# Attention scores from two float32r parts, with two heads in the row halves of the TensorE array

## The reference

```python
q = _split_heads(Q @ W_Q.T)
k = _split_heads(K @ W_K.T)
v = _split_heads(V @ W_V.T)
scores = jnp.einsum('bhqd,bhkd->bhqk', q, k) / jnp.sqrt(jnp.float32(DK))   # DK = 16
scores = jnp.where(mask == 0, -jnp.inf, scores)                            # layer 0 only
weights = jax.nn.softmax(scores, axis=-1)
attn = jnp.einsum('bhqk,bhkd->bhqd', weights, v)
```

## Time and profile before

| what | value |
|---|---|
| median of three runs | 1252.16 us |
| span of the profiled execution | 1261.0 us |
| TensorE busy | 1114.1 us, 88% |
| VectorE busy | 834.2 us, 66% |
| ScalarE busy | 644.9 us, 51% |
| GpSimd busy | 211.6 us, 17% |
| DMA, SyncE's queue | 128.03 MB, 33.3% of 16 engines' span |
| mean granted TensorE clock | 0.946 |

### The profile page before, as it was taken

How to read it: one execution, slowest core, us unless ns; L and a number is a source line. 1 busy time by engine, 2 the same in 40 slices (tenths; PEclk the granted TensorE clock), 3 DMA queues, 4 the chain that set the end, 5 groups by cost and what they waited for, 6 DMA issues and landing times. The chain is left out here.

```text
span 1261.0 us, 17546 instructions
## 1 busy us (share of the span) xinstructions
PE 1114.1 (88%) x5578; PEld 545.0 (43%) x5578; DVE 834.2 (66%) x2112; ACT 644.9 (51%) x1341; POOL 211.6 (17%) x273
## 2 busy tenths in 40 slices
PE   7889999999897999999859999996979999998480
PEld 4423344434452334333446666664523333335350
DVE  5877777776577898898752222225789898868622
ACT  3446666666442776767513333322437767774240
POOL 3310000000242000010211222202410010102244
PEclk9989999999998999999959999998969999999695
DMA  8963312220069334342470220103953223201154
GB/s 252 317 205 87 88 35 81 52 52 1 1 222 274 89 104 116 93 116 62 169 279 29 102 91 29 27 22 106 330 184 107 76 64 85 64 15 67 30 155 142
DMA packets 102433, 139.38 MB, mean 111 GB/s; under 512 B 10756, under 2 KB 84360, under 8 KB 100936
## 3 DMA queue, kind: packets, MB, share of 16 engines
q1 hardware_dynamic: 98264, 128.03, 33.3%
q0 software_dynamic: 4080, 10.23, 3.0%
HBM read 86.30 MB, written 52.17 MB: 110 GB/s over the span
## 5 line engine op out<-in xcount | busy, mean ns | idle before, releaser
L888 ACT ACTIVATE r<-ps 128x512 f32<-128x512 f32 x768 | 427.8, 600 | 209.4 <-PE ps L973 126.5
L377 DVE TENSOR_REDUCE m<-ps 128x1 f32<-128x512 f32 x512 | 320.7, 683 | 38.1 <-PE ps L960 38.1
L973 PE MATMUL ps<-r 99*128 99x512 bf16 x768 | 293.6, 387 | 11.5 <-ACT r L888 5.8
L960 PE MATMUL ps<-r 96*128 96x512 bf16 x720 | 282.9, 394 | 15.0 <-DVE m L377 5.0
L990 PE MATMUL ps<-r 128*32 128x512 f32 x1536 | 199.4, 606 | 5.9 <-ACT r L888 3.3
L373 DVE CUSTOM_DVE_ANT_0 r<-ps,r 128x512 bf16<-128x512 f32 x256 | 166.6, 688 | 55.2 <-PE ps L960 54.6
L973 PEld LDWEIGHTS ps<-r 99*128 99x128 bf16 x768 | 74.7, 98 | 201.6 <-ACT r L888 114.2
L960 PEld LDWEIGHTS ps<-r 96*128 96x128 bf16 x720 | 71.1, 99 | 110.1 <-DVE m L377 29.1
L864 POOL COPY r<-r 128x256 f32<-128x256 f32 x48 | 19.1, 401 | 526.6 <-PE ps L990 526.6
L977 PE MATMUL ps<-r,identb 128*128 128x512 bf16 x256 | 97.9, 382 | 0.0
L1663 DVE COPY r<-ps 128x512 f32<-128x512 f32 x46 | 31.8, 692 | 90.4 <-PE ps L1710 90.4
(11 more groups left out here) (152 smaller groups left out, 1196.8 us busy)
## 6 DMA issues: line engine op xcount, KB each, us to landing
r<-q_parts SPq DMA_DIRECT2D x48, 384.0 KB, 4.0
r<-k_parts SPq DMA_DIRECT2D x48, 384.0 KB, 5.0
k_parts<-r SPq DMA_DIRECT2D x24, 384.0 KB, 3.2
q_parts<-r SPq DMA_DIRECT2D x24, 384.0 KB, 3.2
r<-in_w SPq DMA_DIRECT2D x16, 512.0 KB, 3.5
r<-in_w SPq DMA_DIRECT2D x8, 1024.0 KB, 14.2
k_parts<-r SPq DMA_DIRECT2D x24, 256.0 KB, 3.2
q_parts<-r SPq DMA_DIRECT2D x24, 256.0 KB, 3.1
```

Source lines behind the costliest of these rows:

```text
L377: ins = dve.tensor_reduce(out, mem.ps[:, bank, :], AX.X, ALU.max)
L888: act.activation(mem.probs[:, u // HG, u % HG, :], ps[:, ST + (UNITS * g + u) % DEEP, :], ACT.Exp, scale=SCALE).then_inc(a.p_exp.sem, 1)
L960: pe.matmul(ps[:, led_bank(n), :], mem.qst[g][0:ROWS, h, t * P:(t + 1) * P], mem.kst[g][0:ROWS, h, :], start=True, stop=True).then_inc(a.s ...
L973: ins = pe.matmul(out, mem.kst[g][0:KROWS, h, kt * P:(kt + 1) * P], mem.qst[g][0:KROWS, h, :], start=True, stop=not a.masked)
```

## The change

```diff
-TERMS = 6
+TERMS = 3
-PARTS = 3
+PARTS = 2
+SIDES = 2
+SIDE = P // SIDES
 def load_stacks(sp, a, b, g):
-        rows = src[b, g * GW:(g + 1) * GW, :, :].rearrange("(h r) t n -> (r t) h n", h=HG)
-        sp.dma_start(dst[0:ROWS, :, :], rows).then_inc(a.stacks[g].sem, 16)
+        rows = src[b, g * GW:(g + 1) * GW, :, :].rearrange("(h j r) t n -> j (r t) h n", h=PAIRS, j=SIDES)
+        for j in range(SIDES):
+            sp.dma_start(dst[j * SIDE:j * SIDE + ROWS, :, :], rows[j]).then_inc(a.stacks[g].sem, 16)
+def led_tile(v):
+    return (v % HG) ^ 1, v // HG
+def stack_of(stack, h, rows):
+    j = h % SIDES
+    return stack[j * SIDE:j * SIDE + rows, h // SIDES, :]
     def rest(b, n):
-        dve.scalar_tensor_tensor(mem.res[n % 2], ps[:, QK_BANK + n, :], bias_of(a, n), mem.parts[n][:, 0, :],
+        dve.scalar_tensor_tensor(mem.parts[n][:, 1, :].bitcast(F32R), ps[:, QK_BANK + n, :], bias_of(a, n),
-    def third(b, n):
...
-    def second_part(b, n):
...
     def parts(b, n):
-        sp.wait_ge(a.lo.sem, a.lo.at(b, n + 1))
+        sp.wait_ge(a.r1.sem, a.r1.at(b, n + 1))
...
     def scores(g, v, n, used):
-        h, t = v // T, v % T
+        h, t = led_tile(v)
-        pe.matmul(ps[:, led_bank(n), :], mem.qst[g][0:ROWS, h, t * P:(t + 1) * P],
-                  mem.kst[g][0:ROWS, h, :], start=True, stop=True).then_inc(a.s_ps.sem, 1)
+        pe.matmul(ps[:, led_bank(n), :], stack_of(mem.qst[g], h, ROWS)[:, t * P:(t + 1) * P],
+                  stack_of(mem.kst[g], h, ROWS), start=True, stop=True).then_inc(a.s_ps.sem, 1)
     def transposed_scores(b, g, u, first):
-        ins = pe.matmul(out, mem.kst[g][0:KROWS, h, kt * P:(kt + 1) * P], mem.qst[g][0:KROWS, h, :],
-                        start=True, stop=not a.masked)
         if a.masked:
-            ins = pe.matmul(out, mem.identb[:, :], mem.mbT[:, batch, kt, :].rearrange("p b n -> p (b n)"),
-                            start=False, stop=True)
+            pe.matmul(out, mem.identb[:, :], mem.mbT[:, b, kt, :], start=True, stop=False)
+        pe.matmul(out, stack_of(mem.kst[g], h, KROWS)[:, kt * P:(kt + 1) * P], stack_of(mem.qst[g], h, KROWS),
+                  start=not a.masked, stop=True).then_inc(a.st_ps.sem, 1)
     def split(G):
...
-        dve.tensor_copy(mid, mem.mres[:, :, :]).then_inc(a.cut.sem, 1)
-        dve.tensor_tensor(lo, mem.mres[:, :, :], mid, ALU.subtract).then_inc(a.cut.sem, 1)
```

More of the change, by code:

```diff
@@ L31 @@
 U32 = mybir.dt.uint32
+F32R = mybir.dt.float32r
 ALU = mybir.AluOpType
@@ L168, in __init__ @@
         self.cT = self.cT2[1]
-        self.parts = [take(self.r1, PARTS * S // 2, [PARTS, S], BF16) for _ in range(2 * C)]
-        self.res = [take(self.r1, S, [S]) for _ in range(2)]
+        self.parts = [take(self.r1, PARTS * S, [PARTS, S]) for _ in range(2 * C)]
         self.junk = [take(self.r1, S // 2, [S], BF16) for _ in range(8)]
@@ L211, in __init__ @@
         at[0] = gate_from
[L212 to L216, removed]
+        self.xg = [take(self.r3, D, [D]) for _ in range(DEPTH)]
+        self.xT = [take(self.r3, C * P, [C, P]) for _ in range(2)]
+        self.mid = take(self.r3, F, [F])
+        self.midT = take(self.r3, FT * P, [FT, P])
+        self.y = [take(self.r3, D, [D]) for _ in range(DEPTH)]
+        assert at[0] <= logits_from + T * D
         self.yg = self.r2[:, 0:NT * D].rearrange("p (t d) -> p t d", t=NT)
@@ L249, in __init__ @@
         self.r1 = sig("r1", 2 * C, 2 * C)
-        self.midp = sig("midp", 2 * C)
-        self.lo = sig("lo", 2 * C, 2 * C)
-        self.stored = [sig(f"stored{n}", 16 * PARTS, 16 * PARTS) for n in range(2 * C)]
+        self.stored = [sig(f"stored{n}", 32, 32) for n in range(2 * C)]
         self.v_ps = sig("v_ps", 2)
@@ L262, in __init__ @@
             self.shift_ones = sig("shift_ones", 16)
-        self.stacks = [sig(f"stacks{s}", 32) for s in range(NG)]
-        self.shift = sig("shift", 16)
+        self.stacks = [sig(f"stacks{s}", 64) for s in range(NG)]
+        self.shift = sig("shift", 16 * SIDES)
         self.s_ps = sig("s_ps", UNITS)
@@ L368, in maximum @@
     mem = a.mem
-    h, t = v // T, v % T
-    out = mem.m[:, t, h:h + 1]
+    h, t = led_tile(v)
+    at = h // SIDES * T + t
+    out = mem.m[:, G % 2, h % SIDES, at:at + 1]
     if a.masked:
@@ L532, in scale @@
         pool.tensor_tensor(mem.rstd[:, :], mem.var[:, :], mem.neghalf[:, :], ALU.pow).then_inc(a.scale[last].sem, 1)
-    def third(b, n):
-        pool.wait_ge(a.midp.sem, a.midp.at(b, n + 1))
-        pool.tensor_tensor(mem.parts[n][:, 2, :], mem.res[n % 2], mem.parts[n][:, 1, :],
-                           ALU.subtract).then_inc(a.lo.sem, 1)
     def body(b, ahead):
[L541 to L544, removed]
+        if ahead is not None:
+            scale(ahead)
     if a.norms == 2:
@@ L793, in shift @@
         sp.wait_ge(a.m_sb.sem, a.m_sb.at(G, 1))
-        sp.dma_start(mem.qst[g][ROWS:KROWS, :, :].rearrange("a h (t n) -> a (h t) n", t=T), mem.mT[:, :])\
-          .then_inc(a.shift.sem, 16)
+        for j in range(SIDES):
+            rows = mem.qst_in[g][j * SIDE + ROWS:j * SIDE + KROWS, :, :].rearrange("a h (t n) -> a (h t) n", t=T)
+            sp.dma_start(rows, mem.mT[j * MROWS // SIDES:(j + 1) * MROWS // SIDES, :]).then_inc(a.shift.sem, 16)
     def body(b, first, last):
```

153 lines of the change are left out of this document (76 added, 77 removed).

## The result

The changed kernel took 1282.35 us (median of four runs, 1279.39 to 1284.97), the kernel before beside it 1251.92 us. The ratio is 1.0236, with a 95% interval of 1.0213 to 1.0259: slower. The forecast was 1230 us, so its sign was wrong. The profiled execution after took 1280.02 us with a span of 1278.3.

The account below looks back on a forecast made before the run. TensorE was taken to bound the kernel, by little in sa0 and xa1, by 16 us in xa0. -40.6 (sa0, xa1) + 24 (xa0) - 6 (projections) = -22.6 us: 1252.2 becomes 1230 us, range 1155 to 1340.

Parts of the forecast that it names:

- Pace and overlap: Score matmuls: float32r goes at bfloat16 pace and opposite row halves stream together, 0.22 us a pair instead of 0.44.
- The rivals of half pace and of no overlap: A score pair takes 0.43 us: 1327 us without overlap, 1337 at half pace; chance of either one 0.28.
- The block of products as it was: Float32 passes of 0.43 us: a block costs TensorE 1.08 us, xa0's double block 1.94, form changes included.
- The form in xa0: Form changes (0.22 us) and loads (0.09) raise xa0's unit from 0.654 to 0.746 us: +24 us.
- some 3: The 28 units of xa0 without a score tile add some 3 us.
- A full wait of 0.33: Upper bound for changing the tile form both ways, waiting for a matmul's end: 0.33 us where 0.22 was charged.
- xa1 and sa0: TensorE's batch there falls to 40.7 us (pairs 14.0, blocks 17.3, rest 9.4); the two stages save 40.6 us in all.
- VectorE becomes the bound: In sa0 and xa1 VectorE instead of TensorE sets the batch: 45.4 us in xa1, 48.1 in sa0.
- I add 1.5 for stalls: In sa0 and xa1, 1.5 us a batch for stalls behind blocks of products: 47 us in xa1, 49.5 in sa0.
- ScalarE at 38 stays below: In sa0 and xa1 ScalarE, at 38 us a batch, stays below VectorE, the bound.
- Projections: Shorter path to the stores against more loads and a second shift: -2 us in each of three stages, -6 (bounds -16, +6).
- The mask stage gives the gain back, and more: Rival: sa0 and xa1 gain 41 us, but xa0 loses 74 with changes and loads at upper ends; 1279 us, chance 0.14.

Follow-up runs that it names:

- Run 2: The changed kernel with each score tile in the same row half as its unit's transposed tile; 1424.25 us.
- run 11: The changed kernel with sa0's and xa1's maxima, and from each stage's second group their exponentials, over 256 of 512 columns; 1242.42 us.
- run 6: The changed kernel with the maxima of sa0 and xa1 over 256 of 512 columns; 1258.23 us, ratio 1.0.
- run 10: The changed kernel again, unedited; 1286.18 us, ratio 1.0247.
- Run 3: The changed kernel without the mask matmul in the transposed scores of xa0; 1239.63 us, ratio 0.989.
- the later products: The changed kernel with each block of products one unit later (LATE 3 for 2) in all three attentions; 1288.49 us, ratio 1.0271.
- run 9: The kernel before with the masks of two of each four heads in xa0 moved from TensorE to GpSimd; 1262.34 us, ratio 1.0044.

## Why the prediction was wrong

**Pace and overlap: right.** A float32r pair in opposite halves starts at the same hundredth of a microsecond and the next pair comes 0.24 us later, where 0.22 was taken. Run 2 shows that the halves do it. No run shows the 0.218 that the sum takes for a pair; what was measured in its place is this 0.24. Each float32r matmul of 512 columns stands in the trace as one record, where 512 columns of float32 took 0.86 us: two matmuls of 256 columns, which stand as four records. The rivals of half pace and of no overlap are out.

**The block of products as it was: right.** The kernel before writes four products a block and the trace has eight records. In xa0, at clock 1.00, a double block has 16:

```profile
206.74 0.38 PE L960 MATMUL ps<-r 96*128 96x512 bf16 x1
207.05 1.92 PE L990 MATMUL ps<-r 128*32 128x512 f32 x16
...
208.90 0.39 PE L973 MATMUL ps<-r 99*128 99x512 bf16 x1
```

The next matmul starts 1.85 us after it where a single block had 0.99: the eight records more are 0.86, 0.43 a pass, and the 0.13 beyond the streaming is there once for a block, not once for a pass. With the 0.31 ahead, as in the earlier trace rows, the double block costs the 1.94 that the prediction took.

**The form in xa0: right for a unit, too small for the last 28.** A unit was forecast at 0.746 us and measures 0.75; a batch at 72 and it took 72.4 at clock 1.00. From xa0's first mark to sa0's first the loss was 31.1 us for +24 and the projection's share. Two things lie beyond it. One is the clock: the fifth and thirteenth groups, at 0.91, lost 2.9 and 3.0 us where the same group of the third batch, at 1.00, lost 1.3, and the first two, at 0.53 and 0.92 (before 0.63 and 1.00), lost 6.6 where the next two lost 2.0; that is 8 us. The other is the last 28 units, which have no score tile. The forecast has "some 3" for them, but its own terms (0.218 + 0.22 + 0.04 + 0.218 for 0.436) give 7.3, and at clock 1.00 such a unit takes 0.74 us, 353.02 to 353.76 here, and the last 28 together took 30.2 us where it was 21.7, from the first start to the last:

```profile
353.02 0.38 PE L981 MATMUL ps<-r,identb 128*128 128x512 bf16 x1
353.33 0.50 PE L982 MATMUL ps<-stacks 50*128 50x512 f32 x1
353.76 0.39 PE L981 MATMUL ps<-r,identb 128*128 128x512 bf16 x1
```

A full wait of 0.33 with hidden loads would make the unit 0.218 + 0.33 + 0.218 = 0.77 (that bound has 0.21 for the distance of two starts, which is 0.22 in the earlier trace rows; with it the bound is 0.32). The trace agrees that a change costs: 0.32 and 0.43, less 0.22 for the mask and 0.24 for the pair, leave 0.29 us, where 0.31 was taken for form and loads. It also shows the loads: behind a change of form the load starts with its matmul (231.62 for both records of L981, 231.94 for both of L982), while before, behind a matmul of the same form, it started 0.22 ahead (989.09 for 989.31, L960). How much of the 0.29 is the form and how much the loads no run takes apart.

**The step that failed is "xa1 and sa0": TensorE's batch of 40.7 us, and from it "VectorE becomes the bound".** In run 11, with both other engines relieved, a batch of xa1 still takes 48.0 us, nearly all of it TensorE's own order. Three terms of the 40.7 were too small:
- A pair is 0.24, not 0.218, 64 times: 1.4 us.
- A block of products was left at 1.08. Its old form trip was between 128-row tiles and 32-column tiles; now a pair stands on either side. By the timeline of run 11: 0.33 ahead, 0.99, and 0.34 behind, where two pairs are 0.24 each: (0.33 - 0.24) + 0.99 + (0.34 - 0.24) = 1.18, 0.10 more, 16 times: 1.6 us.
- A turn is 0.59 for 0.44 (six of them), a step of the output projection 1.06 for 0.86 (four), the turning of the maxima 0.26 for 0.06 (four): 2.5 us, less 0.4 because the round trips of these 14 cost 0.19 and not 0.22: 2.1 us.

That is 5.1 of the 7.3 us; the rest is about what TensorE still waits for exponentials in run 11 (0.5 and 0.2 us in the first group of the next batch). The price of one round trip, 0.22, was sized well for a pair among other pairs (0.19). What I counted wrongly is what stands between the trips: beside 64-row pairs, a block, a turn and a step each take longer than before.

**"I add 1.5 for stalls" failed too.** With TensorE at 48 and VectorE at 45.5 us in one order, neither hides the other: xa1 goes 48.0 (run 11), 49.9 with full exponentials (run 6), 51.8 with full maxima (run 10, clock 1.00). In sa0 it is 49.7, 51.5 and 54.3, where 49.5 was forecast. VectorE is not the bound but adds 1.9 to 2.8 us on top of one, and ScalarE another 1.8 to 1.9. "ScalarE at 38 stays below" has the same fault.

**The clock was not in the sum.** At 1.00 xa1's batch is 51.8, 1.2 below before. The changed kernel ran six of ten such batches at 0.91 or 0.94, which cost 2.1 to 3.6 us each. So at full clock the change gains about 1 us a batch in sa0 and xa1 (54.4 and 55.0 became 53.5 and 54.3), not 5.4 and 6.0, and in xa1 the clock took back more than that. The last 28 units, put at no change, took 21.3 and 21.2 us where it was 19.6.

**Projections: more than forecast, and within its bounds.** By the starts of the transposed scores, the first of xa0 comes at 74.4 us for 76.6, and from the last of xa0 to the first of sa0 it is 73.4 for 78.5: -2.2 and -5.1 where -2 was forecast for each. Part of the second may be hidden behind xa0's longer end, which no run took apart. The -5.6 ahead of xa1 (311.1 for 316.7) holds the experts too. That the stores keep the DMA engines full holds in part: before, the DMA share was 1.02 from 35 to 50 us (xa0), 0.57 from 360 to 370 and 1.01 from 370 to 380 (sa0), and 0.97 and 1.07 in 880 to 900 and 900 to 915 (xa1).

**The named rival.** "The mask stage gives the gain back, and more" had 1279 us. That it lies near the result is chance, for it came there by another way: it had the gain of 41 us in sa0 and xa1 and 74 lost in xa0, and neither happened. Run 3 parts the two: with the mask gone, this rival leaves the gain whole, some 40 us below before, and 14 were measured, which xa0 alone accounts for.

What stays open: what makes the clock fall in the changed kernel's xa1, beyond that it does so in some batches and not in others of one execution. TensorE is not busy in 2.3 us of a batch at 1.00 now (49.5 of 51.8) and was in 0.7 before (52.3 of 53.0); whether that matters no run tests.

## What to carry to other kernels

Before a tile form is narrowed to save streaming, list every neighbour of the new form in TensorE's order: each block of another form between them pays on both sides, here 0.2 to 0.3 us a trip, whatever the pair itself gains. An engine that the sum says is "the bound" is only that if the others are well below; at 48 against 45 in one in-order loop the batch was 52. To find what one engine's order costs alone, relieve the others (half the columns) and read its batch, which here was 48 us where the plan had 41. Compare batches of equal granted clock, or an edit gets the credit for it, as the later products did.

## What the runs showed of the hardware

- A 50-row tile in rows 0 to 63 and a 48-row tile in rows 64 to 127 started together in the trace (231.19 and 231.19); in the same half they started 0.35 apart.
- TensorE was busy for 60 us without a gap, in half-row tiles and products, and the granted clock stood at 0.50 throughout (run 2, one execution). It had fallen at 526.9 us, with TensorE busy in 5.0 of the 6.9 us ahead, and rose at 632.8.
- In xa1 of the changed kernel it fell to 0.50 for 10.2 us and rose again. TensorE was busy in 5.75 of the 6.7 us ahead of the fall (one wait of 0.93 us for an exponential, up to 1004.4) and in 10.19 of the 10.24 us at 0.50:

```profile
1000.00:1003.00 3.00, 3.00 (x22) 1.36 (x23) 2.72 (x7) 2.09 (x4) 0.00 (x0) 1.00 0.31 96
1003.00:1006.72 3.72, 2.75 (x18) 0.78 (x17) 3.09 (x6) 2.28 (x4) 0.00 (x0) 1.00 0.68 159
1006.72:1016.96 10.24, 10.19 (x39) 3.60 (x39) 6.13 (x13) 5.56 (x12) 0.40 (x1) 0.50 0.21 45
1016.96:1020.00 3.04, 3.04 (x22) 1.25 (x20) 2.97 (x8) 1.92 (x4) 0.00 (x0) 1.00 0.02 5
```

- A float32r weight load of 128 columns took 0.19 us (192 and 195 ns mean, L982 and L967), where the bfloat16 load it replaced took 98 ns; in run 11's batch at clock 1.00 it was 185 ns. The prediction had taken 141.
- GpSimd multiplied 128x512 float32 by bfloat16 in place in 1.17 us, and VectorE's maxima beside it kept their 0.69 us (run 9). Two operations of VectorE that read no scores from PSUM were slower beside it: the conversion of the mask took 0.57 us for 0.42, and the last step of `split` 0.44 for 0.20.
